# Moving three small pieces of VectorE work in an attention and mixture-of-experts kernel: value factors, gated bias, and statistics of updated rows

## The reference

```python
x = x + jnp.tanh(g_xattn[0]) * xattn(ctx_1024, layernorm(x), ...)
x = x + jnp.tanh(g_ffn[0]) * ffn(layernorm(x), ...)
```

## Time and profile before

| | |
|---|---|
| median of 3 runs | 918.78 us (918.63 to 922.09) |
| profiled execution | 916.49 us |
| its span, first to last instruction | 914.8 us |
| mean granted TensorE clock | 0.991 |
| PE busy | 872.6 us (95%) |
| PEld busy | 811.4 us (89%) |
| DVE busy | 693.6 us (76%) |
| ACT busy | 655.4 us (72%) |
| POOL busy | 677.4 us (74%) |

### The profile page before, as it was taken

The page is one execution under the profiler, slowest core; times in us unless marked ns, Lnnn a source line. Parts: engine busy times, 40 slices in busy tenths (PEclk is TensorE's granted clock), DMA queues, the critical chain, the costliest instruction groups (busy, mean ns, idle before and its releaser), DMA issues. The chain is left out here.

```text
span 914.8 us, 21998 instructions
## 1 busy us (share of the span) xinstructions
PE 872.6 (95%) x6288; PEld 811.4 (89%) x6288; DVE 693.6 (76%) x1849; ACT 655.4 (72%) x1699; POOL 677.4 (74%) x1027
## 2 busy tenths in 40 slices
PE   4899999999999999999999999999999969999985
PEld 3799999999999999999999999999999968999985
DVE  5767668787888778887778787877787768768764
ACT  5777878777877878787878787878787761455642
POOL 3776667686868686868686868686977785777576
PEclk9999999999999999999999999999999999999998
DMA  7665668544445535364534454435464457798792
GB/s 220 141 153 140 171 137 169 144 91 103 87 107 84 113 78 117 73 116 81 110 84 109 87 110 82 114 76 114 76 123 79 95 160 249 237 345 250 215 293 86
DMA packets 255702, 123.98 MB, mean 136 GB/s; under 512 B 213740, under 2 KB 235487, under 8 KB 255584
## 3 DMA queue, kind: packets, MB, share of 16 engines
q1 hardware_dynamic: 244864, 101.18, 49.2%
q0 software_dynamic: 8064, 21.25, 6.4%
q10 hardware_dynamic: 2656, 0.14, 0.2%
HBM read 39.87 MB, written 33.63 MB: 80 GB/s over the span
## 5 line engine op out<-in xcount | busy, mean ns | idle before, releaser
L512 POOL TENSOR_TENSOR pn<-prob,rinv 128x333 f32<-128x333 f32 x256 | 186.5, 753 | 133.9 <-DVE rinv L1061 133.0
L519 POOL TENSOR_TENSOR pl<-pn,ph 128x333 f16<-128x333 f32 x256 | 201.8, 812 | 0.0
L667 ACT ACTIVATE prob<-ps_s,nmax 128x333 f32<-128x333 f32 x128 | 69.2, 541 | 99.7 <-DVE nmax L868 95.5
L661 ACT ACTIVATE ph<-prob,rinv 128x333 f16<-128x333 f32 x256 | 134.7, 590 | 0.5 <-DVE rinv L1061 0.4
L1236 PE MATMUL ps_ar<-pth,v_hi 128*128 128x256 f16 (+1 forms) x384 | 106.2, 276 | 2.2 <-DVE o_lo L1028 1.2
L862 DVE SCALAR_TENSOR_TENSOR v_lo<-ps_g,vscale,v_hi 128x512 f16<-128x512 f32 (+1 forms) x96 | 71.6, 746 | 47.7 <-ACT v_hi L653 46.3
L1236 PE MATMUL ps_ar<-pth,v_lo 128*128 128x256 f16 (+1 forms) x384 | 104.5, 272 | 0.0
L1236 PE MATMUL ps_ar<-ptl,v_hi 128*128 128x256 f16 (+1 forms) x384 | 104.3, 272 | 0.0
L667 ACT ACTIVATE prob<-ps_g,nmax 128x333 f32<-128x333 f32 x128 | 69.0, 539 | 29.1 <-DVE nmax L868 29.1
L1236 PE MATMUL ps_k<-ln_hi,w_hi 128*128 128x334 f32 x256 | 82.0, 320 | 3.0 <-DVE ln_lo L1145 3.0
L1236 PE MATMUL ps_k<-ln_hi,w_lo 128*128 128x334 f32 x256 | 81.3, 318 | 0.0
(11 more groups left out here) (390 smaller groups left out, 3203.1 us busy)
## 6 DMA issues: line engine op xcount, KB each, us to landing
xin<-by_first SPq DMA_DIRECT2D x32, 130.0 KB
xin<-by_second SPq DMA_DIRECT2D x14, 260.0 KB
x_all<-in_x_dram SPq DMA_DIRECT2D x7, 512.0 KB, 4.5
rows_turned<-x2t_hi SPq DMA_DIRECT2D x13, 256.0 KB, 2.4
rows_turned<-x2t_lo SPq DMA_DIRECT2D x13, 256.0 KB, 2.4
w_hi<-rows_turned SPq DMA_DIRECT2D x13, 256.0 KB, 3.3
w_lo<-rows_turned SPq DMA_DIRECT2D x13, 256.0 KB, 4.1
x_all<-by_first SPq DMA_DIRECT2D x12, 260.0 KB, 4.1
```

The lines of the kernel that those rows point to most:

```text
L512: pool.tensor_tensor(pn[:, i, 0:KEYS], prob[:, h % 2, i, 0:KEYS], rinv[:, h % 2, i:i + 1].to_broadcast([P, KEYS]), ALU.mult).then_inc(norm ...
L519: pool.tensor_tensor(pl[:, h % 2, i, 0:KEYS], pn[:, i, 0:KEYS], ph[:, h % 2, i, 0:KEYS], ALU.subtract).then_inc(pl_ready, 1)
L661: act.activation(ph[:, par, i, 0:KEYS], prob[:, par, i, 0:KEYS], ACT.Identity, scale=rinv[:, par, i:i + 1]).then_inc(ph_ready, 1)
L667: act.activation(prob[:, h % 2, i, 0:KEYS], ps_s[i][:, 0:KEYS], ACT.Exp, bias=nmax[:, h % 2, i:i + 1], accum_out=rsum[:, i:i + 1]).then_in ...
```

## The change

It moves three calls in DVE's stream and leaves all instructions the same. `value_factors()` goes from before the first step to after the step of head 2 of batch 0. `tgbo` goes from after the step of head 0 to after the step of head 4 of batch 0. `x2_statistics(b - 1)` in head 3 of batches 1 to 15 goes from behind the value piece `v_lo` (the last work of that step) to ahead of it, right behind `keep_info`.

```diff
--- before.py
+++ after.py
@@ -1072,6 +1072,8 @@
                     sigmoids(b)
                 if h == 3 and third:
                     keep_info(b)
+                if h == 3 and first:
+                    x2_statistics(b - 1)
                 if h == 6 and first:
                     shifts2(b)
                 if h == 6 and second:
@@ -1111,8 +1113,6 @@
                                              op1=ALU.add).then_inc(x2_ready, 1)
                 if h == 2 and third:
                     destinations(b)
-                if h == 3 and first:
-                    x2_statistics(b - 1)
                 if h == 4 and first:
                     x2_aggregate()
 
@@ -1194,10 +1194,11 @@
             q_part(0, 0, 0)
             split_lo(4)
             v_piece(0, 0)
-            value_factors()
             for h in range(HEADS):
                 step(0, h, 0)
-                if h == 0:
+                if h == 2:
+                    value_factors()
+                if h == 4:
                     dve.wait_ge(tg_ready, 1)
                     dve.tensor_scalar(tgbo[:, :], bo[:, :], tg[:, 0:1], None, ALU.mult).then_inc(tg_ready, 1)
             for b in range(1, ROUTED + 1):
```

## The result

| | before | after |
|---|---|---|
| median of runs timed side by side | 918.63 us (5 runs, 916.94 to 922.09) | 911.54 us (5 runs, 909.63 to 912.22) |
| profiled execution, span | 916.49, 914.8 us | 912.22, 910.4 us |

The ratio is 0.9919, with a 95% interval of 0.9896 to 0.9943: 7.4 us faster (5.2 to 9.6). The forecast was 5.5 us, 913.3 with a range from 911.5. The ratio applied to the 918.78 of the forecast gives 911.3, just under that range; the median itself is just inside. The two profiled spans differ by only 4.4 us.

The account below looks back on a forecast made before the run. PE was taken as the bound, busy nearly throughout, so DVE edits count only through PE's waits. Gains of 2.6 and 2.9 us made 5.5 us, from a median of 918.78 to 913.3 us, range 911.5 to 916.5.

Parts of the forecast that it names:

- Edits 1 and 2: Batch 0: moving value_factors() and tgbo later starts head 2's scores 3.59 us earlier, worth 2.6 us after losses.
- The two waits of PE: Batch 0, before the scores of heads 1 and 2: waits for q_lo shrink to about 0.5 and 0.1 us.
- the chain has nothing else late: Batch 0, head 0's maximum to PE's next scores: one chain, so head 1's scores start 1.74 us earlier.
- The landing: Moved pieces in heads 2 and 4 of batch 0 cost PE 0.96 us in all, tgbo nothing more.
- The rival of the full price: Heads 2 and 4: landing costs 1.5 and 0.7 us, gain only 4.3 us, 914.5 us; chance 0.17.
- Edit 3: Head 3 of later batches: statistics ahead of v_lo close twelve waits for q_lo, 12 x 0.25, 2.9 us.
- The slower rival: Head 4 picks held by POOL make PE lose 1.15 us in each of 13 batches, 928.3 us; chance 0.04.
- the pick pair: Two small DVE operations in head 4, reached 0.7 us earlier; if held by POOL, DVE is 1.4 us later.
- The sum: Whole kernel: 2.6 us from the front plus 2.9 us from the later batches, 5.5 us faster.
- at the other end to 911.5 for the scatter of a median: Whole kernel: low end of the range set at 911.5 us to allow for a median's scatter.

Follow-up runs that it names:

- e9_act: Full change plus one-input tgs, value factors and batch 1 statistics ahead of v_lo, and bvs made by ScalarE; 0.9916 of the kernel before, median 908.42 us.
- e4_bias: Kernel before with only tgbo moved, to behind head 4, value factors left in front; ratio 0.9969, 2.8 us faster.
- e1_stats: Kernel before with only x2_statistics moved ahead of v_lo in head 3; ratio 0.9967, 3.0 us faster.
- e3_factors: Kernel before with only value_factors() moved, to after head 2, tgbo left behind head 0; ratio 1.0006, no gain seen.
- b3_look: Kernel before, no edit, one more profile; head 2 took 6.52 us.
- e6_tgs: Kernel before with tgs as a product by a per-partition scalar, one SBUF input; one profile, 710.96 us from first scores to batch 15, head 7.
- b4_look: Kernel before, no edit, one of five more profiles, which took 709.64 to 711.08 us from first scores to batch 15, head 7.

## Why the prediction was right or wrong

- **Edits 1 and 2 at the front: right.** Forecast 3.59 us at head 2's scores, 3.69 measured (14.10 - 10.41). The two waits of PE were forecast at 0.5 and 0.1 us and are 0.59 and 1.53; the second was wrong without effect, since PE ran head 1 at full clock and waited, as the text allowed. That the chain has nothing else late held for the two edits together; with edit 1 alone the clock took the gain away.
- **The landing: right.** tgs and bvs forecast with 0.5 and 0.75 us, measured 0.43 and 0.79. From head 3 to head 6 the kernel took 16.25 us before and 17.30 after: 1.05 given back, forecast 0.96. Head 3 lost 0.46 us (forecast 0.4) and head 4 another 0.57, with idles of PE of 0.21 and 0.32 us where 0.4 to 0.6 were forecast; the weight loads in front of them show 0.49 and 0.60. It was VectorE held up by GpSimd: with tgs on one SBUF input and bvs on ACT nothing is given back (e9_act). The rival of the full price is out; tgbo cost nothing (e4_bias).
- **Edit 3: right in mechanism and place, and in size.** Forecast 2.9 us (12 x 0.25 is 3.0), 3.14 measured between batch 1 and batch 15 in the first profiles, 3.12 in e1_stats and 2.99 by the means: head 4 became 0.23 to 0.26 us shorter in ten of the twelve batches, 0.17 and 0.12 in the other two. The slower rival did not come about: DVE reaches the pick pair before POOL's next operation, and the pair takes 0.21 and 0.15 us where the second took 0.77.
- **The sum: 5.5 forecast, 5.7 on the ruler, 5.1 in each of two later timings, 7.4 in the first.** The intervals of all three hold 5.7. What failed is the step "at the other end to 911.5 for the scatter of a median". It put the low end only 0.8 us below what the terms give at best (918.78 - 6.5 = 912.3) and 1.8 below the forecast. In its place the runs showed this: the interval of the first ratio alone is 2.2 us to either side, the medians of the kernel before in five measurements lie between 916.96 and 919.0, and its single runs between 913.97 and 922.09. The mechanism needs no fourth term.
- **Where the scatter comes from, as far as the record goes.** Of 69 later runs of the kernel before, the 19 with a mean granted clock of 0.988 or 0.989 took 919.5 us in the median, the 16 with 0.994 or more 915.8. So the scatter of single runs goes with the granted clock, 3.7 us between these groups; that the clock is its whole cause is not shown, and in which stage it fell is known only for profiled runs. The extra of the first timing lies on the side of before: the full change took 911.54 and 911.49 us in the first two measurements, the kernel before 918.63 and 916.96. Whether chance or something real raised it stays open, since no clock is on record for those runs of before; the half clock in head 2 would make some 0.2 us of it, by six profiles.
- **Anchoring.** I noted that the profiled run lay 2.3 us under the median but did not ask why. Its head is the shortest of six profiles, and the two profiled spans (4.4 us apart) understate the change for that reason: the first scores start 1.50 us later in the profile after than in that before.

## What to carry to other kernels

An engine that looks fully busy can still be late by a quarter of a microsecond in each pass, as PE was here in twelve batches; the waits of its weight loads show it when the busy time does not. Put work that nobody waits for ahead of the instruction that waits for another engine, not behind it, and keep from such a slot every small VectorE operation that a long GpSimd operation can hold up, or give it to ScalarE. Before a few tenths of a per cent are forecast, take several profiles of the kernel before: the spread of its head and tail, and of its medians, is the least width of the range. And where an idle of PE is shortened, look at the next one: in e3_factors a shorter idle ahead of head 1 came with a longer one ahead of head 2, and the half clock that followed took the gain.

## What the runs showed of the hardware that I had not expected

- The granted clock was 0.50 for about 3 us after some idles of PE, and not after others of the same length. Ahead of head 1, idles of 1.97 to 2.30 us were followed by it in seven profiles, one of 2.30 us (e4_bias) was not, nor were those of 1.68 us and less. It cost nothing there. But where head 1 ran at 1.00 and tgbo still held up VectorE, PE's idle ahead of head 2 grew to 3.39 to 3.42 us, and the 0.50 then stood in head 2, where it cost 1.5 us: so in b3_look, e3_factors and e6_tgs. Idles of 1.84 to 1.97 us at that place were not followed by it. So the length of the last idle alone does not decide; what does was not tried.
- The range products ahead of the first scores (128x512) start 0.23 us apart in the profile before and 0.43 us apart in that after. The granted clock reads 1.00 over both stretches, so the lower speed is read from the spacing: the ratio is about that of products of head 1 at a granted clock of 0.50 and of 1.00 (128x334: 0.28 us apart in b4_look, 0.15 in e4_bias). From the first of these products to the first scores it takes 3.09 us before and 4.29 after, 1.2 of the 1.5 us by which the first scores differ. The timelines of PE, before and then after:

```profile
18.11 0.39 PE L1403 MATMUL ps_ar<-x2t_lo,gwide 128*128 128x512 f32 x1
18.34 0.40 PE L1403 MATMUL ps_ar<-o_hi,gwide 128*128 128x512 f32 x1
```

```profile
19.09 0.63 PE L1404 MATMUL ps_ar<-o_hi,gwide 128*128 128x512 f32 x1
19.52 0.63 PE L1404 MATMUL ps_ar<-o_lo,gwide 128*128 128x512 f32 x1
```

- A VectorE product of 5 or 3 columns by a per-partition scalar is held until GpSimd's operation ends, as one of 8 is (5 columns for 1.82 us under a w_lo, 3 columns for 0.78 us under a pn); one of a single column is not (0.22 us beside a w_lo). When the first held operation is freed, the next one takes over the wait.
